# Graph network, mixer and routed experts on one core: the counting of the choices at seven turns' distance

## The chip, the cores and the metric

One NeuronCore of a Trainium2 chip runs the whole program in one launch. The metric is the device time of one execution, from its first to its last instruction, in microseconds. Three executions of the kernel before took 2806.68, 2806.97 and 2810.98 us; the median is 2806.97 us.

## What is computed

6250 nodes with 256 features pass three blocks, each added to the nodes; everything is float32:

```python
xn = _layernorm(x, axis=-1)
x = x + _L0_gnn_ref(xn, ...) + _L0_mix_ref(xn[None], ...)[0]
x = x + _L0_ffn_ref(_layernorm(x, axis=-1)[None], ...)[0]
# in _L0_ffn_ref, for E = 32 experts of hidden size 64:
logits = xf @ router_w.T + router_b
idx = jnp.argmax(logits, axis=-1)
h = relu(einsum('nd,ndh->nh', xf, W1[idx]) + b1[idx])
out = relu(einsum('nh,nhd->nd', h, W2[idx]) + b2[idx])
```

The first block averages edge features by node and puts them through two products; the second has four layers of linear attention and a feed-forward part; the third sends each node to the one expert with the highest logit.

## The kernel before, in words

The 6250 nodes stand as 50 tiles of 125; two tiles are a pair, and there are `GROUPS` = 25 pairs. The program goes through these stages: sorting and scattering of the edges beside the first mixer layer, the four mixer layers, the sums over the edges, then from about 2400 us **the routing loop**, and from about 2660 us the experts, which read whole pages of 128 tokens of one expert from a table in memory.

The routing loop is what the change touches. It is a pipeline written out by hand: each engine has a loop over turns i of its own (line 2433 for TensorE, 1951 for VectorE, 898 for GpSimd, and one for ScalarE), and `live(d)` says whether pair i-d exists. Work on pair i-d in turn i is at "distance d". The engines meet through semaphores only, and each handles its instructions in program order.

- Distance 0 to 2: `graph_input`, `graph_means`, `graph_transpose`, `graph_high`, `graph_low` bring a pair's inputs into the form `cT`; `graph_up(i-2, 0)` and `graph_up(i-2, 1)` make two chunks of hidden values (16 matmuls `cT_*,g_*` each) on TensorE. ScalarE makes `ghid` and its rounded part `ghh_hi`, VectorE the rest `ghh_lo` (`graph_hidden_low`, line 1834).
- Distance 3: `graph_down` (24 matmuls `g_*,ghh_*`). Distance 4: `graph_residual` adds the result to `res` (line 1839) and takes moments; GpSimd takes the root, VectorE the shift, ScalarE the normalised `zt`.
- Distance 5: TensorE transposes `zt` (line 2020), ScalarE copies it to `zT` (`route_copy`, line 1196). In ScalarE's turn this copy stands between `graph_relu(i-2, 0)` and `graph_hidden_high(i-2, 0)`.
- Distance 6: TensorE makes the logits (`rwT,zT`, eight matmuls), VectorE adds the bias (`logit`, line 1862), finds the largest and its index, and, as the last instruction of its turn, writes the choice as zeros and a one: `chosen` (line 1881). Four buffers `chosen[g % 4]` are in rotation.
- Distance 8: **the counting.** `rank_tokens` on TensorE adds up in a bank of PSUM how many tokens before each have chosen which expert (five small matmuls with `tri_r`, `ones_r` and `rest_r`); it stands at the head of TensorE's turn. VectorE reads the counts (`route_rank`: `limits`, line 1891, and `picks`, line 1892), computes the pages held (`route_pages`, line 1898), the ends of the pages, and picks the values for each token (`route_pick`, `route_sum`).
- Distance 9 on GpSimd: `token_slots` turns them into row numbers `fpos_i`, and `scatter_tokens` writes the pair's two tiles into the table by two indirect DMAs (line 894). For the last pairs, from `SLOTS_LATE` on, VectorE computes the row numbers itself, in the same turn (`route_slots`, last line 1943).

The order that these give to TensorE's turn, and what the counting products wait for:

```python
pe.wait_ge(n_chosen, g + 1)
pe.wait_ge(n_counted, COUNTED + g)
```

`n_chosen` is raised by `route_chosen(g)`, `n_counted` by `route_pages(g-1)`, since the bank keeps adding up and is read in between. The DMA of the pages' kinds on SP (line 738) waits for all 50 scatters, and the experts wait for that. VectorE's loop has 32 turns; from turn 27 on no new hidden chunks are left, and the last turns hold routing alone.

Of the kernel before, what the change touches and what calls it, by code (L numbers as in the profile page):

```python
# [21 lines left out]
GROUPS = TILES // PAIR  # L22
# [30 lines left out]
PAGE_RND = 8388608.0 * PAGE  # L53
FILL = 4
CHOICES = 4
SLOTS_LATE = GROUPS - 7
FSEGS = (N + EXP * (PAGE - 1)) // PAGE
RIN = 6

# [56 lines left out]
def build(nc, x, src, edge_attr, u, gW1, gb1, gW2, gb2, Wq, Wk, Wv, Wo, bo, ln1_g, ln1_b, mW1, mb1, mW2, mb2,  # L116
# [9 lines left out]
    with ctx:  # L126
# [409 lines left out]
        def pair(t, g, n=D):  # L536
            return t[:, bass.ds(g * PAIR, PAIR), 0:n]
# [208 lines left out]
        def _(pool):  # L746
# [145 lines left out]
            def scatter_tokens(g):  # L892
                for t in range(PAIR * g, PAIR * (g + 1)):
                    nc.gpsimd.indirect_dma_start(
                        out=tokens_sorted, out_offset=bass.IndirectOffsetOnAxis(ap=fpos_i[:, t:t + 1], axis=0),
                        in_=res[:, t, :], in_offset=None).then_inc(f_scat, 16)

            for i in range(4, GROUPS + 9):
                if i < GROUPS + 4:
                    pool.wait_ge(n_ve, i - 3)  # L900
                    nc.gpsimd.tensor_tensor(pair(res, i - 4, D + 1)[:, :, D], gve[:, :], tail_half[:, :], ALU.pow).then_inc(n_root, 1)
                if i == 9:
                    pool.wait_ge(blank_written, 32 + 16 * (KC + 1) * (FSEGS // FILL))
                if i >= 9:
                    token_slots(i - 9)
                    scatter_tokens(i - 9)

            for n in range(FSEGS):
                pool.wait_ge(f_row, n + 1)
# [340 lines left out]
        def _(dve):  # L1250
# [637 lines left out]
            def route_rank(g):  # L1888
                dve.wait_ge(n_ranked, g + 1)
                dve.wait_ge(n_placed, g)  # L1890
                step_(nc.vector.tensor_scalar(limits[:, :], PQT[0:P, PAIR * EXP:(PAIR + 1) * EXP], (PAGE - 1) / 2.0, PAGE_RND, ALU.add, ALU.add))
                step_(nc.vector.tensor_tensor(picks[:, :, 4, :], PQT[0:P, 0:PAIR * EXP].rearrange("p (j e) -> p j e", j=PAIR),
                                              chosen[g % CHOICES][:, :, :], ALU.mult))
# [7 lines left out]
            def route_ends(g):  # L1901
                stepped()
                step_(nc.vector.tensor_tensor_scan(ends[:, g % 2, :], ones[0:P, 0:EXP], fresh[:, :], ends[:, (g + 1) % 2, EXP - 1:EXP], ALU.mult, ALU.add))
# [44 lines left out]
            graph_x(0)  # L1948
            dve.wait_ge(gw_hi, 3)
            nc.vector.tensor_tensor(g2[1][:, :, :], raw_g2[:, :, :], f32(g2[0][:, :, :]), ALU.subtract).then_inc(gw_lo, 1)  # L1950
            for i in range(1, GROUPS + 8):
                def live(d):
                    return 0 <= i - d < GROUPS
                if live(4):
                    graph_residual(i - 4)
                if live(0):
                    graph_sums(i)
                if live(2):
                    graph_hidden_low(i - 2, 0)
                if live(0):  # L1960
                    graph_x(i)
                if live(4):
                    graph_shift(i - 4)
                if live(8):
                    route_rank(i - 8)
                if live(6):
                    route_logits(i - 6)
                if live(8):
                    route_pages(i - 8)
                if live(6):  # L1970
                    route_best(i - 6)
                if live(8):
                    route_ends(i - 8)
                if live(1):
                    graph_low(i - 1)
                if live(8):
                    route_grown(i - 8)
                if live(8):
                    route_book(i - 8)
                if live(6):  # L1980
                    route_index(i - 6)
                if live(8):
                    route_pick(i - 8)
                if live(2):
                    graph_hidden_low(i - 2, 1)
                if live(8):
                    route_sum(i - 8)
                    if i - 8 >= SLOTS_LATE:
                        route_slots(i - 8)
                if live(6):  # L1990
                    route_chosen(i - 6)

# [23 lines left out]
        def _(pe):  # L2016
# [413 lines left out]
            for k in range(KC):  # L2430
                nc.tensor.transpose(PQ[:, k * EXP:(k + 1) * EXP], rw_in[:, k * 128:(k + 1) * 128], ident[0:EXP, 0:EXP])
            nc.tensor.transpose(PQ[0:EH, KC * EXP:(KC + 1) * EXP], fb1_r, ident[0:EXP, 0:EXP]).then_inc(gcol_pe, 1)
            for i in range(2, GROUPS + 8):
                def live(d):
                    return 0 <= i - d < GROUPS
                if live(8):
                    rank_tokens(i - 8)
                if live(2):
                    graph_up(i - 2, 0)
                if live(6):  # L2440
                    route_logits(i - 6)
                if live(5):
                    route_transpose(i - 5)
                if live(2):
                    graph_up(i - 2, 1)
                if live(1):
                    graph_transpose(i - 1)
                if live(3):
                    graph_down(i - 3, 0)
                    graph_down(i - 3, 1)  # L2450
# [66 lines left out]
```

## Time and profile before

| | |
|---|---|
| median of three executions | 2806.97 us |
| the profiled execution: its own time | 2808.5 us |
| its span (first to last instruction recorded) | 2806.5 us |
| mean granted clock of TensorE | 0.968 |
| TensorE busy | 2623.6 us (93%) |
| VectorE busy | 2140.3 us (76%) |
| ScalarE busy | 1600.6 us (57%) |
| GpSimd busy | 1747.9 us (62%) |

Busy shares are means over stages with different limits. For one stage, the view of stretches gives each engine's busy time in it, and the timeline gives the single instructions in order; a bracket behind a row there tells how long the engine had been idle before it, and what released it. PE is TensorE, DVE VectorE, ACT ScalarE and POOL GpSimd. A granted clock of 1.00 is 2.4 GHz, 0.50 is 1.2 GHz.

### The profile page before, as it was taken

The page shows a single profiled execution, that of the slowest core. Times are in us where ns is not written, and L with a number is a line of the kernel's source. Part 1 is how long each engine was busy: PE and PEld are TensorE (multiplying, and loading weights), DVE is VectorE, ACT ScalarE, POOL GpSimd, SP SyncE. Part 2 cuts the span into 40 slices and gives each one's busy share as a digit, 9 for nine tenths or more (in the row PEclk, how much of TensorE's full clock was granted, in tenths as well). Part 3 has the DMA queues.
Part 4 walks back from the last instruction along what each step waited for, and adds up shares of the span by engine and source line. Part 5 has one row for each costly group of instructions (what it writes and reads, how often), then busy time and mean ns, then how long its engine had stood idle before and what let it go on. Part 6 is the DMA issues. An engine that isn't in the chain of part 4 may idle for free.

```text
span 2806.5 us, 57791 instructions
## 1 busy us (share of the span) xinstructions
PE 2623.6 (93%) x19601; PEld 2462.4 (88%) x19601; DVE 2140.3 (76%) x4920; ACT 1600.6 (57%) x3127; POOL 1747.9 (62%) x1751
## 2 busy tenths in 40 slices
PE   4888999999989999999999999989999999899798
PEld 3667899999979999998999999979998998899665
DVE  8988677777767777777677777778888888689754
ACT  0545466666646666664566666544444444677375
POOL 2145577777688877777887777745555555056555
PEclk7999999999999999999999999999999999899799
DMA  6012444334242322222422222234333332232252
GB/s 131 30 49 47 118 93 93 86 88 92 44 113 64 73 55 65 63 56 67 103 66 60 59 66 55 59 100 123 89 85 88 88 89 69 59 84 60 57 157 74
DMA packets 281805, 218.66 MB, mean 78 GB/s; under 512 B 171344, under 2 KB 220564, under 8 KB 281515
## 3 DMA queue, kind: packets, MB, share of 16 engines
q1 hardware_dynamic: 230444, 173.33, 23.8%
q0 software_dynamic: 51072, 41.66, 7.3%
q8 instruction: 160, 2.62, 0.4%
q14 instruction: 129, 1.06, 0.1%
HBM read 137.05 MB, written 80.92 MB: 78 GB/s over the span
## 4 chain that ended last, share of the span: by engine, by line
PE 66%; DVE 16%; issue 7%; POOL 7%; ACT 2%; DVEq 1%; DMA 1%; SPq 0%; POOLq 0%; ACTq 0%
PE bank L412 60%; POOL edges_sorted L812 5%; PE bank L2020 4%; DVE hidh_lo L1453 3%; DVE xh L1417 2%; DVE scr L1327 2%; DVE oh L1650 1%; PE bank L2488 1%; DVEq L1629 1%; POOL ehl L828 1%; DVE bn L1408 1%; DMA queries<-qn 1%; DVE bn_x L1253 1%; DVE res L1425 1%; POOL r L790 1%
## 5 line engine op out<-in xcount | busy, mean ns | idle before, releaser
L812 POOL DMA_INDIRECT edges_sorted<-staging,pos_i x850 | 1076.0, 1266 | 246.5 <-issue 230.1
L958 ACT ACTIVATE hid<-bank,b1p 128x250 f32<-128x250 f32 x800 | 331.6, 466 | 317.7 <-PE bank L412 315.5
L412 PE MATMUL bank<-w_hi,hidh_hi 128*125 128x256 f32 x1600 | 473.0, 296 | 23.1 <-DVE hidh_lo L1453 23.1
L412 PE MATMUL bank<-h_hi,w_hi 128*128 128x250 f32 x1600 | 479.3, 300 | 2.5 <-DVE h_lo L1437 2.4
L1453 DVE TENSOR_TENSOR hidh_lo<-hid,hidh_hi 128x500 fp32r<-128x500 f32 x400 | 319.7, 800 | 179.5 <-ACT hidh_hi L964 173.0
L412 PE MATMUL bank<-w_hi,hidh_lo 128*125 128x256 f32 x1600 | 454.2, 284 | 0.0
L412 PE MATMUL bank<-w_lo,hidh_hi 128*125 128x256 f32 x1600 | 452.6, 283 | 0.0
L412 PE MATMUL bank<-h_hi,w_lo 128*128 128x250 f32 x1600 | 448.8, 280 | 0.0
L412 PE MATMUL bank<-h_lo,w_hi 128*128 128x250 f32 x1600 | 445.3, 278 | 0.0
L412 PEld LDWEIGHTS bank<-w_hi,hidh_hi 128*125 128x125 f32 x1600 | 300.9, 188 | 32.1 <-DVE hidh_lo L1453 29.3
L964 ACT CAST hidh_hi<-hid 128x500 fp32r<-128x500 f32 x400 | 243.8, 610 | 122.6 <-PE bank L412 116.2
L412 PEld LDWEIGHTS bank<-h_hi,w_hi 128*128 128x128 f32 x1600 | 304.3, 190 | 6.5 <-DVE h_lo L1437 4.0
L412 PEld LDWEIGHTS bank<-h_lo,w_hi 128*128 128x128 f32 x1600 | 305.5, 191 | 1.9
L412 PEld LDWEIGHTS bank<-w_lo,hidh_hi 128*125 128x125 f32 x1600 | 300.5, 188 | 2.1
L412 PEld LDWEIGHTS bank<-h_hi,w_lo 128*128 128x128 f32 x1600 | 302.1, 189 | 0.0
L412 PEld LDWEIGHTS bank<-w_hi,hidh_lo 128*125 128x125 f32 x1600 | 300.3, 188 | 0.0
L790 POOL TENSOR_TENSOR r<-ve,minus_half 125x2 f32<-125x2 f32 x175 | 135.1, 772 | 217.1 <-DVE ve L1413 214.5
L828 POOL TENSOR_TENSOR ehl<-staging,ehl 128x512 fp32r<-128x512 f32 x103 | 137.6, 1336 | 148.5 <-ACT ehl L1050 136.2
L1650 DVE TENSOR_TENSOR oh<-iota_node,kb 128x1000 fp32r<-128x1000 f32 x153 | 190.3, 1244 | 43.5 <-POOL kb L823 43.3
L971 ACT COPY qT<-bank 128x500 f32<-128x500 f32 x100 | 57.7, 577 | 279.9 <-PE bank L2020 279.9
L412 PE MATMUL bank<-xh,ek 125*128 125x256 f32 x800 | 195.6, 390 | 6.7 <-DVE acc L1550 4.1
L412 PE MATMUL bank<-mmat,qT 128*125 128x256 f32 x800 | 191.8, 383 | 3.6 <-issue 3.6
(300 smaller groups left out, 6653.0 us busy)
## 6 DMA issues: line engine op xcount, KB each, us to landing
staging<-edges_sorted SPq DMA_DIRECT2D x103, 260.0 KB, 2.7
staging<-in_edge_attr SPq DMA_DIRECT2D x50, 531.2 KB
queries<-qn SPq DMA_DIRECT2D x100, 250.0 KB
qin<-queries SPq DMA_DIRECT2D x100, 250.0 KB
edges_sorted<-staging,pos_i POOLq DMA_INDIRECT x850
rows_in<-edges_sorted SPq DMA_DIRECT2D x50, 260.0 KB, 2.6
yin<-tokens_sorted SPq DMA_DIRECT2D x80, 130.0 KB, 2.1
tokens_sorted<-tri SPq DMA_DIRECT2D x40, 256.0 KB
```

The source lines that it names most:

```text
L412: return nc.tensor.matmul(o, left, right, start=start, stop=stop, skip_group_check=True)
L790: nc.gpsimd.tensor_tensor(o[:, :], ve[:, :], minus_half[:, :], ALU.pow).then_inc(done, 1)
L812: nc.gpsimd.indirect_dma_start(out=edges_sorted, out_offset=bass.IndirectOffsetOnAxis(ap=pos_i[:, i:i + 1], axis=0), in_=stage[:, slot, j, ...
L828: nc.gpsimd.tensor_tensor(ehl[n % 4][:, :, EA + 2:2 * EA + 2], rows_in[n % RIN][:, :, 0:EA], f32(ehl[n % 4][:, :, 0:EA]), ALU.subtract).th ...
L958: a = nc.scalar.activation(hid[c % 2][:, j, :], chunks(PH[c % 2])[:, j, :], ACT.Gelu, bias=b1p[:, 2 * c + j:2 * c + j + 1])
L964: nc.scalar.copy(hidh[c % 2][0][:, :, :], hid[c % 2][:, :, :]).then_inc(f_hi, 1)
L971: nc.scalar.copy(qT[:, :, :], chunks(PQT)).then_inc(q_copied, 1)
L1327: nc.vector.copy_predicated(pos_f[:, part], mask.bitcast(U16), PH[u % 2][0:P, 0:width]).then_inc(e_acc, 1)
L1417: a = nc.vector.tensor_scalar(o[:, j, :], res_row(PAIR * g + j), mv[:, j, 0:1], r[:, j:j + 1], ALU.subtract, ALU.mult)
L1453: nc.vector.tensor_tensor(hidh[c % 2][1][:, :, :], hid[c % 2][:, :, :], f32(hidh[c % 2][0][:, :, :]), ALU.subtract).then_inc(f_lo, 1)
L1650: nc.vector.tensor_tensor(oh[n % 4][:, :, :], iota_node[:, :].unsqueeze(1).to_broadcast((128, SEGR, P)), kb[:, n % 4, :].unsqueeze(2).to_b ...
L2020: a = nc.tensor.transpose(o[0:128, c, j * n:(j + 1) * n], i[:, j, c * 128:(c + 1) * 128], ident[0:n, 0:n])
```

## The change

The counting and all that stands behind it go from distance 8 to distance 7 on TensorE and VectorE, the slots and scatters from 9 to 8 on GpSimd; the loops of these three are one turn shorter. In TensorE's turn `rank_tokens` stands behind `graph_up(i-2, 0)` now, ahead of the logits. `SLOTS_LATE` goes from 18 to 19, so VectorE computes the row numbers of six pairs, and GpSimd those of nineteen. ScalarE's and SP's programs are the same.

```diff
-SLOTS_LATE = GROUPS - 7
+SLOTS_LATE = GROUPS - 6
...
-            for i in range(4, GROUPS + 9):
+            for i in range(4, GROUPS + 8):
...
-                if i == 9:
+                if i == 8:
                     pool.wait_ge(blank_written, 32 + 16 * (KC + 1) * (FSEGS // FILL))
-                if i >= 9:
-                    token_slots(i - 9)
-                    scatter_tokens(i - 9)
+                if i >= 8:
+                    token_slots(i - 8)
+                    scatter_tokens(i - 8)
...
-            for i in range(1, GROUPS + 8):
+            for i in range(1, GROUPS + 7):
...
-                if live(8):
-                    route_rank(i - 8)
+                if live(7):
+                    route_rank(i - 7)
                 if live(6):
                     route_logits(i - 6)
...
-            for i in range(2, GROUPS + 8):
+            for i in range(2, GROUPS + 7):
                 def live(d):
                     return 0 <= i - d < GROUPS
-                if live(8):
-                    rank_tokens(i - 8)
                 if live(2):
                     graph_up(i - 2, 0)
+                if live(7):
+                    rank_tokens(i - 7)
                 if live(6):
                     route_logits(i - 6)
```

`route_pages`, `route_ends`, `route_grown`, `route_book`, `route_pick`, `route_sum` and `route_slots` go from `live(8)` and `i - 8` to `live(7)` and `i - 7` in the same way, at their places in VectorE's turn.

**TensorE, a turn in the middle of the loop.** `chosen0` to `chosen3` are the four buffers of choices; `cT_*,g1_*` are products of `graph_up`, `g2_*,ghh*` of `graph_down`, `rwT,zT` the logits. Before, the last products of `graph_down` are followed by the counting, and that by `graph_up`:

```order
L412 MATMUL bank6<-g2_lo,ghh1_hi 125x256
L412 MATMUL bank6<-g2_hi,ghh1_lo 125x256
L412 MATMUL bank2<-chosen3,rest_r 125x64
L412 MATMUL bank2<-chosen3,ones_r 125x32
L412 MATMUL bank2<-chosen0,tri_r 125x64
L412 MATMUL bank2<-chosen0,ones_r 125x64
L412 MATMUL bank2<-chosen0,ones_r 125x32
L412 MATMUL bank4<-cT_hi,g1_hi 128x250
L412 MATMUL bank4<-cT_lo,g1_hi 128x250
```

With the change the counting stands behind the first half of `graph_up` and ahead of the logits:

```order
L412 MATMUL bank4<-cT_hi,g1_hi 128x250
L412 MATMUL bank4<-cT_hi,g1_lo 128x250
L412 MATMUL bank2<-chosen3,rest_r 125x64
L412 MATMUL bank2<-chosen3,ones_r 125x32
L412 MATMUL bank2<-chosen0,tri_r 125x64
L412 MATMUL bank2<-chosen0,ones_r 125x64
L412 MATMUL bank2<-chosen0,ones_r 125x32
L412 MATMUL bank3<-rwT,zT 125x32 x4
L2020 MATMUL bank1<-ident,zt 128x125 x4
```

These are the five products of pair 12 both times: they stand sixteen matmuls later in the turn now, and one turn earlier.

**TensorE, the last turns.** Before, the counting of pair 22 and the last logits, those of pair 24:

```order
L412 MATMUL bank2<-chosen1,rest_r 125x64
L412 MATMUL bank2<-chosen1,ones_r 125x32
L412 MATMUL bank2<-chosen2,tri_r 125x64
L412 MATMUL bank2<-chosen2,ones_r 125x64
L412 MATMUL bank2<-chosen2,ones_r 125x32
L412 MATMUL bank3<-rwT,zT 125x32 x4
L412 MATMUL bank2<-chosen2,rest_r 125x64
```

With the change, the same place:

```order
L412 MATMUL bank2<-chosen2,rest_r 125x64
L412 MATMUL bank2<-chosen2,ones_r 125x32
L412 MATMUL bank2<-chosen3,tri_r 125x64
L412 MATMUL bank2<-chosen3,ones_r 125x64
L412 MATMUL bank2<-chosen3,ones_r 125x32
L412 MATMUL bank3<-rwT,zT 125x32 x4
L412 MATMUL bank2<-chosen3,rest_r 125x64
```

The last logits stand behind the counting of pair 23 now, whose choice is buffer `chosen3`.

**VectorE, the end of the loop.** The last row numbers of the old turn 31, and what is left out behind them:

```order
 L1943 TENSOR_TENSOR fpos_i<-late_slots 125x2
-L1891 TENSOR_SCALAR limits<-bank 125x32
-L1892 TENSOR_TENSOR picks<-bank,chosen 125x2x32
-L1898 TENSOR_SCALAR book<-limits 125x32
-L1899 SCALAR_TENSOR_TENSOR fresh<-limits,book 125x32
-L1903 SCALAR_TENSOR_TENSOR ends<-ones,ends,fresh 125x32
-L1907 SCALAR_TENSOR_TENSOR fresh<-fresh,ends 125x32
-L1912 TENSOR_TENSOR book<-fresh,book 125x32
-L1917 TENSOR_TENSOR picks<-book,chosen 125x2x128
-L1927 TENSOR_REDUCE picked<-picks 125x10
-L1935 TENSOR_TENSOR late_slots<-picked 125x2 x2
-L1936 TENSOR_TENSOR late_slots<-picked 125x2
```

The loop's last turn is gone: the counting of pair 24 is VectorE's turn 31, in the place of pair 23's.

## Rows read from the trace of the kernel before

**Rows 1.** Busy time by stretch: us, each engine's busy us, PEclk, DMA share, GB/s
```profile
2250.00:2300.00 50.00, 46.20 (x378) 44.53 (x378) 42.61 (x64) 23.17 (x46) 28.93 (x33) 1.00 0.32 87
...
2550.00:2600.00 50.00, 50.00 (x451) 50.00 (x450) 45.63 (x176) 36.77 (x85) 31.12 (x63) 1.00 0.21 59
...
2639.00:2648.00 9.00, 3.00 (x18) 2.78 (x18) 8.07 (x48) 0.00 (x0) 6.02 (x6) 0.50 0.28 73
```

**Rows 2.** Timeline, TensorE, turn 19: start us, duration us, instruction, count
```profile
2553.04 0.96 PE L412 MATMUL bank<-rwT,zT 128*125 128x32 f32 x8
...
2553.83 0.63 PE L2020 MATMUL bank<-ident,zt 125*128 125x125 f32 x4
...
2559.65 0.19 PE L412 MATMUL bank<-chosen,rest_r 125*125 125x64 bf16 x1
...
2559.91 0.36 PE L412 MATMUL bank<-cT_hi,g_hi 128*128 128x250 f32 x1
...
2561.87 0.96 PE L412 MATMUL bank<-rwT,zT 128*125 128x32 f32 x8
```

**Rows 3.** Timeline, TensorE, the logits of turn 25
```profile
2606.02 0.96 PE L412 MATMUL bank<-rwT,zT 128*125 128x32 f32 x8
```

**Rows 4.** Timeline, ScalarE, turn 19 (in brackets: idle before, and releaser)
```profile
2554.50 0.58 ACT L1196 COPY zT<-bank 128x500 f32<-128x500 f32 x1 [0.42 <-PE bank L2020]
...
2554.97 0.61 ACT L1183 CAST ghh_odd_hi<-ghid 128x500 fp32r<-128x500 f32 x1
```

**Rows 5.** Timeline, VectorE, turn 19
```profile
2555.61 0.68 DVE L1834 TENSOR_TENSOR ghh_odd_lo<-ghid,ghh_odd_hi 128x500 fp32r<-128x500 f32 x1 [0.25 <-ACT ghh_odd_hi L1183]
...
2561.77 0.23 DVE L1881 TENSOR_TENSOR chosen<-iota_seg,res 125x64 bf16<-125x64 f32 x1
```

**Rows 6.** Timeline, VectorE, turns 25 to 32
```profile
2614.53 0.23 DVE L1881 TENSOR_TENSOR chosen<-iota_seg,res 125x64 bf16<-125x64 f32 x1
...
2623.00 0.23 DVE L1881 TENSOR_TENSOR chosen<-iota_seg,res 125x64 bf16<-125x64 f32 x1
...
2630.61 0.68 DVE L1839 TENSOR_TENSOR res<-res,bank 125x512 f32<-125x512 f32 x1
...
2637.86 0.23 DVE L1881 TENSOR_TENSOR chosen<-iota_seg,res 125x64 bf16<-125x64 f32 x1
...
2638.46 0.23 DVE L1862 TENSOR_TENSOR logit<-bank,rb_b 125x64 f32<-125x64 f32 x1
...
2638.60 0.17 DVE L1898 TENSOR_SCALAR book<-limits 125x32 f32<-125x32 f32 x1
...
2647.45 0.23 DVE L1881 TENSOR_TENSOR chosen<-iota_seg,res 125x64 bf16<-125x64 f32 x1
...
2647.59 0.18 DVE L1891 TENSOR_SCALAR limits<-bank 125x32 f32<-125x32 f32 x1
...
2650.80 0.16 DVE L1943 TENSOR_TENSOR fpos_i<-late_slots 125x2 int32<-125x2 f32 x1
...
2654.29 0.16 DVE L1943 TENSOR_TENSOR fpos_i<-late_slots 125x2 int32<-125x2 f32 x1
```

**Rows 7.** Timeline, TensorE, turns 27 to 30
```profile
2623.88 0.38 PE L412 MATMUL bank<-g_hi,ghh_hi 128*125 128x256 f32 x1 [1.33 <-DVE res L1839]
...
2628.34 0.19 PE L412 MATMUL bank<-chosen,rest_r 125*125 125x64 bf16 x1
...
2636.61 1.07 PE L2020 MATMUL bank<-ident,zt 125*128 125x125 f32 x4
...
2638.92 0.28 PE L412 MATMUL bank<-chosen,rest_r 125*125 125x64 bf16 x1 [1.24 <-DVE book L1898]
...
2639.23 0.37 PE L412 MATMUL bank<-chosen,ones_r 125*125 125x64 bf16 x2
...
2639.44 1.87 PE L412 MATMUL bank<-rwT,zT 128*125 128x32 f32 x8
```

**Rows 8.** Timeline, GpSimd, the scatter of the last pair
```profile
2654.75 1.19 POOL L894 DMA_INDIRECT tokens_sorted<-res,fpos_i  x1 [0.75 <-DVE fpos_i L1943]
```

More of the change, by code:

```diff
@@ L1963, in _ @@
                     graph_shift(i - 4)
-                if live(8):
-                    route_rank(i - 8)
+                if live(7):
+                    route_rank(i - 7)
                 if live(6):
                     route_logits(i - 6)
-                if live(8):
-                    route_pages(i - 8)
+                if live(7):
+                    route_pages(i - 7)
                 if live(6):
                     route_best(i - 6)
-                if live(8):
-                    route_ends(i - 8)
+                if live(7):
+                    route_ends(i - 7)
                 if live(1):
                     graph_low(i - 1)
[L1976 to L1979, printed above, removed]
+                if live(7):
+                    route_grown(i - 7)
+                if live(7):
+                    route_book(i - 7)
                 if live(6):
                     route_index(i - 6)
-                if live(8):
-                    route_pick(i - 8)
+                if live(7):
+                    route_pick(i - 7)
                 if live(2):
                     graph_hidden_low(i - 2, 1)
[L1986 to L1989, printed above, removed]
+                if live(7):
+                    route_sum(i - 7)
+                    if i - 7 >= SLOTS_LATE:
+                        route_slots(i - 7)
                 if live(6):
@@ L2432, in _ @@
             nc.tensor.transpose(PQ[0:EH, KC * EXP:(KC + 1) * EXP], fb1_r, ident[0:EXP, 0:EXP]).then_inc(gcol_pe, 1)
-            for i in range(2, GROUPS + 8):
+            for i in range(2, GROUPS + 7):
                 def live(d):
                     return 0 <= i - d < GROUPS
-                if live(8):
-                    rank_tokens(i - 8)
                 if live(2):
                     graph_up(i - 2, 0)
+                if live(7):
+                    rank_tokens(i - 7)
                 if live(6):
```

## The prediction

> **What bounds the kernel now.** I read the stretches of 50 us first. From 2450 to 2600 us the routing loop runs, and in such a stretch TensorE is busy 50.00 of 50 us at a granted clock of 1.00, while VectorE has 45.63 [rows 1]. So a turn costs what TensorE issues in it. The marks of one turn show the length: the logits of turn 19 start at 2553.04 and those of turn 20 at 2561.87, 8.83 us later [rows 2]; turn 25 has them at 2606.02 [rows 3], and 52.98 us for six turns is 8.83 again. The loop's end is different: from 2639 to 2648 us VectorE is busy 8.07 of 9.00 us and TensorE 3.00, at half its clock [rows 1]. There the chain of waits runs through VectorE, turn by turn, to the last row numbers at 2654.29; GpSimd waits for these, 0.75 us idle, before its scatter at 2654.75 [rows 6, 8], and the expert pages are loaded behind that. What counts is therefore whether the loop keeps 8.83 us a turn, and when the last row numbers are written.
>
> **The part that decides: a choice needed sooner than it is made.** In the new order the counting products of pair i-7 stand in TensorE's turn i behind `graph_up(i-2, 0)`, where the logits start now. They need the choice of that pair, which VectorE writes as its last routing step of turn i-1. Followed through one turn of the old trace: the logits start at 2553.04, the transposes of `zt` at 2553.83 [rows 2]. ScalarE waited 0.42 us for these and copies at 2554.50, and only behind this copy, at 2554.97, does it round the hidden chunk [rows 4]. VectorE waited 0.25 us for that and starts at 2555.61; from there its own row of work leads to the choice, 2561.77 + 0.23 = 2562.00 [rows 5]. That is 8.96 us after the logits began and 0.13 us after the logits of the next turn began [rows 2]. Before, the choice had a whole further turn; now TensorE stands and waits for it.
>
> It is not a wait paid once, since it closes a ring. Counting products of turn i, then logits and transposes, ScalarE's copy and rounding, VectorE's chain to the choice, counting products of turn i+1. The ring's length is the sum of its pieces: the five counting products, 0.26 us from 2559.65 to 2559.91 [rows 2], now ahead of the logits; the 8.96 us; and the way from VectorE to TensorE, 0.15 us, as VectorE's held pages end at 2638.77 and the products that wait for them start at 2638.92 [rows 6, 7]. The sum is 9.37 us, **0.54 us more than 8.83**. TensorE has 0.54 us less to do than the ring lasts, and stands idle by that in each turn. The choice of pair 1, counted in turn 8, is the first that comes behind counting work on VectorE; so turns 7 to 25 are the ring's marks, 18 lengths: 18 x 0.54 = 9.7 us. The next length is shorter, as VectorE has no new pair to add there: from 2606.02 to the choice at 2614.53 + 0.23 is 8.74 us, with 0.41 it is 9.15, another 0.3 us [rows 3, 6]. From turn 26 the ring is left, but its counting products remain between the chunk and the transposes: 0.26 us. By then VectorE is **10.3 us** late. Were the way to TensorE to cost nothing, the loop's part would be 0.15 x 19 = 2.9 us less; that is the lower bound.
>
> By the Trainium skill, page "Perfetto Trace Analysis", section "Identifying the Most-Contended Engine", the engine to look at is the one with the highest occupancy, TensorE by how long it loads weights; in this stretch its loads fill 50.00 of 50 us [rows 1], the products are the same before and after, and a turn would stay at 8.83 us. That is the rival "no ring" below. The rows agree with the rule for the old order only.
>
> **The end of the loop.** One turn goes: the last row numbers came 2654.29 - 2650.80 = 3.49 us after the ones before [rows 6], work that TensorE's old distance had put into a turn of its own. **-3.49 us.** Against it stand new waits. In turns 29 to 31 VectorE begins with the counts, and the choice they rest on is its last work of the turn before. Before, it went from the choice (2647.45) to `limits` (2647.59) in 0.14 us [rows 6]. Now the choice must end (0.23), reach TensorE (0.15), be counted (2638.92 to 2639.23 + 0.37, so 0.68) [rows 7] and come back (0.04, as ScalarE starts at 2554.50 behind transposes that end at 2553.83 + 0.63) [rows 2, 4]: 1.10 us, **+0.96**. In turns 29 and 30 it is more, because the logits stand behind the counting products in TensorE's queue: they start 0.52 us after these and take 1.87 us at half clock [rows 7], so VectorE has them 0.23 + 0.15 + 0.52 + 1.87 + 0.04 = 2.81 us after the choice began, where it was 2638.46 - 2637.86 = 0.60 [rows 6]: **2 x 2.21 us**. All counts, 4.42 + 0.96 - 3.49 = **+1.9 us**. At full clock (0.96 us for the logits [rows 2], 0.26 for the counts) these turns would wait 1.04, 1.04 and 0.54 us, and the end would gain 0.9 us; the clock in this stretch is 0.50 [rows 1], so I take +1.9.
>
> In turn 27 TensorE does the last `graph_down`, which now also stands behind the counts. It had waited 1.33 us at 2623.88, and lasted until 2628.34 [rows 7]. The choice of turn 26, at 2623.00 + 0.23, comes 10.3 us later, so counts, logits and transposes start at 2633.7 and end 1.9 us (0.26 + 0.96 + 0.63) to 3.5 us (0.52 + 1.87 + 1.07) later; with 4.46 us for the products they are done at 2640.1 to 2641.7. VectorE adds the result at 2630.61 + 10.3 = 2640.9 [rows 6]. Late by 0 to 0.8 us; I take **+0.4**.
>
> **What costs nothing.** GpSimd's slots and both scatters of a pair move one turn earlier, past the root of the next pair; its distance to VectorE's counting is the same, and its last scatter waited for row numbers, not for the queue [rows 8]. Pair 18's slots are computed by GpSimd in place of VectorE, ten instructions for seven, beside a turn that VectorE or TensorE sets; if the cover is gone it is late by these small instructions once. VectorE's turn 7 gets counting work that fills idle time. SP issues the same loads in the same order, and the five products are the same ones.
>
> **Sum.** 10.3 + 0.4 + 1.9 = +12.6 us. Against the profiled execution, 2808.5 us, that is 2821.1; this execution is 1.5 us above the median of the runs, 2806.97, so against that I predict **2819.6 us**.
>
> **Rivals.**
> - *No ring* (the other side: not slower). If the choice is released before its record's end, or VectorE closes up so that TensorE hardly waits, the loop stays at 8.83 us and only the end is left: -3.5 us if its waits are hidden, +1.9 if not, so 2803 to 2809 us, no measurable change. It decides from the point where the ring is within 0.17 us of the turn (18 x 0.17 + 2.3 is 5.4 us). For it speaks only the smallness of 0.54 us; against it that ScalarE's 0.42 and VectorE's 0.25 us of waiting [rows 4, 5] show both standing behind TensorE already.
> - *The clock falls in the loop.* Each idle piece of 0.54 us could take the granted clock down to its half level. Then logits take 0.91 us more, counts 0.26 and transposes 0.44 [rows 2, 7], all on the ring: 1.6 us x 18 = 29 us more, 2849 us; half of that if it falls in some turns. Against it, from 2250 to 2300 us TensorE was busy only 46.20 of 50 us, a larger idle share than 0.54 of 9.37, and the clock stayed at 1.00 [rows 1]. The Trainium skill, "TensorE: Matmul & The Clock Gate", section "A second HAM failure mode: psum-queue depth-cycling", tells of a kernel whose clock went up and down because TensorE paused often and briefly between groups; by it this rival would come true, and the row of 2250 us speaks against it.
> - *The ring is shorter than summed*, with 0.1 to 0.3 us a turn left: 2811 to 2815 us. This joins the forecast, as its lower part.
>
> **How the numbers follow.** The forecast, with the shorter ring, gets 0.77; the clock 0.07; no ring 0.16, of which 0.03 is a gain of over 0.2%, should the end and something behind it gain together. A change within 0.2%, 5.6 us, is about what a measurement of this kernel can't tell from none. So slower 0.84, less 0.02 for a ring so short that it is not told: 0.82; same 0.15; faster 0.03. The range runs from 2811 us (ring 0.3 us, or no way to TensorE and full clock at the end) to 2829 us (the clock falling in a third of the turns): it leaves out most of "no ring" and the upper clock case, together just under 2 in 10.
>
> **What would show it.** Right: the logits of successive turns 9.3 to 9.4 us apart; an idle piece of about 0.5 us of TensorE before each first counting product, released by VectorE's choice; TensorE's busy time near 47 of 50 us at clock 1.00; in the last three turns VectorE idle about 1 us before `limits`, in two of them 1 to 2 us more before `logit`; six late turns of slots on VectorE in place of seven. Wrong: turns still of 8.83 us, or a clock under 0.95 between 2450 and 2600 us.

## The result, and the profile after

| | before | after |
|---|---|---|
| median, us | 2808.93 (2806.68 to 2812.97, 7 runs) | 2818.08 (2815.11 to 2824.44, 7 runs) |
| the profiled execution, us | 2808.5 | 2815.11 |
| its span, us | 2806.5 | 2813.1 |
| mean granted clock of TensorE | 0.968 | 0.972 |

The change makes the kernel slower: a ratio of 1.0034, with an interval of 1.0021 to 1.0047, which is 6 to 13 us. The median is 1.5 us below the predicted 2819.6 us. Part of that closeness is luck: the forecast was 12.6 us on top of a median of 2806.97 us (three executions), and the median of seven is 2808.93 us, so the change costs 9.2 us where 12.6 were forecast. The parts below show where the rest went.

Busy time by stretch, kernel after (us, then TensorE, weight loads, VectorE, ScalarE and GpSimd, granted clock, DMA share, GB/s):

```profile
2550.00:2600.00 50.00, 48.35 (x424) 47.35 (x423) 43.11 (x170) 35.78 (x84) 30.35 (x65) 1.00 0.19 54
2640.00:2650.00 10.00, 3.31 (x17) 2.92 (x17) 7.08 (x43) 0.72 (x2) 3.88 (x4) 0.50 0.20 54
```

From 2550 to 2600 us TensorE was busy 50.00 us before, with 451 matmul instructions [rows 1]; now it is 48.35 us with 424. The clock is 1.00 in both. VectorE and ScalarE do less per stretch as well: no engine is full, and each of them waits for another. The turn shows for whom. Timeline of TensorE, kernel after (in brackets: idle before, and releaser):

```profile
2451.47 0.24 PE L412 MATMUL bank<-chosen,rest_r 125*125 125x64 bf16 x1 [0.36 <-DVE chosen L1881]
...
2554.01 0.28 PE L412 MATMUL bank<-cT_hi,g_lo 128*128 128x250 f32 x1
2554.60 0.24 PE L412 MATMUL bank<-chosen,rest_r 125*125 125x64 bf16 x1 [0.31 <-DVE chosen L1881]
...
2554.91 1.04 PE L412 MATMUL bank<-rwT,zT 128*125 128x32 f32 x8
...
2563.98 0.24 PE L412 MATMUL bank<-chosen,rest_r 125*125 125x64 bf16 x1 [0.32 <-DVE chosen L1881]
...
2610.87 0.24 PE L412 MATMUL bank<-chosen,rest_r 125*125 125x64 bf16 x1 [0.35 <-DVE chosen L1881]
...
2620.05 0.24 PE L412 MATMUL bank<-chosen,rest_r 125*125 125x64 bf16 x1
```

Here `rest_r` is the first of the five counting products. It waits for `chosen` in each turn. From the mark at 2451.47 to the one at 2610.87 are 17 lengths, 159.40 us: **9.376 us a turn**, where it was 8.83 [rows 2, 3].

The way round the ring, after the logits of 2554.91: ScalarE, then VectorE.

```profile
2556.45 0.58 ACT L1196 COPY zT<-bank 128x500 f32<-128x500 f32 x1 [1.29 <-PE bank L2020]
2556.92 0.61 ACT L1183 CAST ghh_odd_hi<-ghid 128x500 fp32r<-128x500 f32 x1
```

```profile
2557.56 0.68 DVE L1834 TENSOR_TENSOR ghh_odd_lo<-ghid,ghh_odd_hi 128x500 fp32r<-128x500 f32 x1 [0.83 <-ACT ghh_odd_hi L1183]
...
2563.69 0.23 DVE L1881 TENSOR_TENSOR chosen<-iota_seg,res 125x64 bf16<-125x64 f32 x1
```

ScalarE's wait before the copy was 0.42 us and is 1.29; VectorE's before `ghh_odd_lo` was 0.25 and is 0.83 [rows 4, 5]. Each engine stands behind the one ahead of it in the ring.

The end of the loop, timeline of VectorE, kernel after:

```profile
2628.53 0.23 DVE L1881 TENSOR_TENSOR chosen<-iota_seg,res 125x64 bf16<-125x64 f32 x1
...
2636.08 0.68 DVE L1839 TENSOR_TENSOR res<-res,bank 125x512 f32<-125x512 f32 x1
...
2643.39 0.23 DVE L1881 TENSOR_TENSOR chosen<-iota_seg,res 125x64 bf16<-125x64 f32 x1
2644.42 0.19 DVE L1891 TENSOR_SCALAR limits<-bank 125x32 f32<-125x32 f32 x1 [0.81 <-PE bank L412]
...
2646.12 0.23 DVE L1862 TENSOR_TENSOR logit<-bank,rb_b 125x64 f32<-125x64 f32 x1 [1.38 <-PE bank L412]
...
2656.72 0.23 DVE L1881 TENSOR_TENSOR chosen<-iota_seg,res 125x64 bf16<-125x64 f32 x1
...
2660.97 0.16 DVE L1943 TENSOR_TENSOR fpos_i<-late_slots 125x2 int32<-125x2 f32 x1
```

Before, `limits` came 0.14 us after the choice began, and `logit` without a wait [rows 6]. Now the three last turns of VectorE wait 0.81 us for the counts, and two of them 1.38 us more for the logits. One turn less stands behind them.

**A ruler that all runs share.** TensorE's transposes of `an` run from the loop's first turn to its 25th. The first and the last of them, and the last `fpos_i`, cut each trace into a loop, an end of the loop, and the rest. The group of these transposes, kernel before, then kernel after (count, ns, first and last start):

```profile
L2367 PE MATMUL bank<-ident,an x50: 270/270/415, 2400.2 to 2609.7; 125*128 125x125 f32 x50
```

```profile
L2367 PE MATMUL bank<-ident,an x50: 270/270/415, 2396.9 to 2614.9; 125*128 125x125 f32 x50
```

The loop lasts 209.5 us before and 218.0 after; the end 44.6 (to 2654.29) and 46.1 (to 2660.97); the rest 152.2 and 152.1. The same numbers for all kernels of this study, each of one profiled execution:

| kernel | loop begins | loop, us | end, us | rest, us | turn, us | ratio to before, interval |
|---|---|---|---|---|---|---|
| before | 2400.2 | 209.5 | 44.6 | 152.2 | 8.83 | 1 |
| after | 2396.9 | 218.0 | 46.1 | 152.1 | 9.38 | 1.0034 (1.0021 to 1.0047) |
| e1_behind_transposes | 2405.3 | 208.2 | 43.0 | 152.2 | 8.84 | 0.9995 (0.9986 to 1.0004) |
| e2_choice_sooner | 2410.5 | 207.9 | 42.5 | 152.3 | 8.83 | 0.9995 (0.9986 to 1.0004) |
| e3_choice_sooner_behind | 2403.5 | 208.1 | 42.2 | 153.6 | 8.84 | 0.9995 (0.9986 to 1.0004) |
| e4_copy_later | 2408.1 | 213.4 | 45.7 | 152.2 | 9.19 | 1.0029 (1.0017 to 1.0041) |
| f1_middle_at_8 | 2408.0 | 207.6 | 44.6 | 152.2 | 8.83 | 1.0002 (0.9992 to 1.0012) |
| f2_head_at_7 | 2403.0 | 296.2 | 49.6 | 153.8 | 12.80 or 14.22, mean 13.67 | 1.0322 (1.0300 to 1.0344) |
| f3_low_later | 2406.3 | 220.6 | 46.4 | 152.2 | 9.43 | 1.0043 (1.0028 to 1.0059) |
| f4_copy_low_later | 2406.5 | 206.9 | 45.3 | 152.3 | 8.83 | 1.0005 (0.9996 to 1.0015) |

The code ahead of the loop is the same in all ten, and yet the loop begins anywhere from 2396.9 to 2410.5 us. A single span is therefore worth little here; the loop, the end and the turn are what the traces tell apart. The kernel before was timed anew beside each set of experiments: 2814.89 us (29 runs) beside e1 to e4, 2815.07 us (21 runs) beside f1 to f4. The ratios of e1 to f4 are to these, that of the change to its own 2808.93 us.

### The profile page after: what moved, and what is told of

The parts are those of the page before. It is cut to its first block, busy times and chain, and to the rows that moved or that the text cites. A ratio compares the mean times of both kernels' runs of the same rounds, so it can differ in the third digit from the quotient of the medians.

```text
span 2813.1 us, 57794 instructions
## 1 busy us (share of the span) xinstructions
PE 2618.4 (93%) x19601; PEld 2454.0 (87%) x19601; DVE 2137.2 (76%) x4913; ACT 1599.5 (57%) x3127; POOL 1746.2 (62%) x1760
## 4 chain that ended last, share of the span: by engine, by line
PE 64%; DVE 19%; issue 8%; POOL 4%; ACT 2%; DVEq 1%; DMA 1%; SPq 0%; ACTq 0%; POOLq 0%
PE bank L412 58%; PE bank L2020 4%; DVE hidh_lo L1453 3%; POOL edges_sorted L812 3%; DVE xh L1417 2%; DVE scr L1327 1%; DVE oh L1650 1%; PE bank L2488 1%; DVEq L1629 1%; POOL ehl L828 1%; DMA queries<-qn 1%; DVE bn L1408 1%; DVE bn_x L1253 1%; DVE res L1425 1%; DVE kmask L1312 1%
## 5 line engine op out<-in xcount | busy, mean ns | idle before, releaser
L1650 DVE TENSOR_TENSOR oh<-iota_node,kb 128x1000 fp32r<-128x1000 f32 x153 | 190.3, 1243 | 42.2 <-POOL kb L823 42.0
```

The source lines that it names most:

```text
L1650: nc.vector.tensor_tensor(oh[n % 4][:, :, :], iota_node[:, :].unsqueeze(1).to_broadcast((128, SEGR, P)), kb[:, n % 4, :].unsqueeze(2).to_b ...
```

## The experiments

Three theories. **Ring**: the counting products need the choice of the turn before, and this closes a ring of 9.37 us. **Place**: the middle of TensorE's turn is itself a bad place for them. **Scatter**: the loop is not the cause; the stages ahead of it differ from one execution to the next, and that is the loss.

**e1: counting behind the transposes.** Against the changed kernel, in TensorE's turn. The distance stays at seven; only logits and transposes leave the ring's way.

```diff
-                if live(7):
-                    rank_tokens(i - 7)
                 if live(6):
                     route_logits(i - 6)
                 if live(5):
                     route_transpose(i - 5)
+                if live(7):
+                    rank_tokens(i - 7)
```

> Distance 7 as in the change, but the counting products stand behind the transposes of zt, 1.42 us later in TensorE's turn (2553.04 to 2553.83 and 0.63 more). Ring theory (choice to counts to logits, transposes, ScalarE, VectorE, choice, 9.37 us long, is what lengthened the turn): the logits and transposes no longer stand behind the choice, which comes 0.13 + 0.15 us after the logits begin and so before its place in the queue. Turns go back to 8.83 us, no idle piece of TensorE in the loop, 0.96 us of wait in each of the last three turns against the 3.49 us turn that is gone: about 0.6 us under the kernel before, near 2808, and 10 us under the change. Place theory (what costs is small products in the middle of TensorE's turn, pushing later work of the turn back): they are still in the middle, turns stay over 9.3 us, 2818. Scatter theory (the loop is not the cause, the stages ahead of it differ from run to run): 2818 again, whatever the turns do.

Measured: 2813.12 us (2810.72 to 2815.74, 11 runs). Timeline of TensorE, e1:

```profile
2540.03 0.19 PE L412 MATMUL bank<-chosen,rest_r 125*125 125x64 bf16 x1
...
2548.87 0.19 PE L412 MATMUL bank<-chosen,rest_r 125*125 125x64 bf16 x1
```

8.84 us apart, with no wait. The choice is still VectorE's last work of the turn, and is counted in the very next; what went is that logits and transposes stand behind the count in TensorE's queue. The end keeps a wait for the counts, and loses the one for the logits:

```profile
2647.81 0.19 DVE L1891 TENSOR_SCALAR limits<-bank 125x32 f32<-125x32 f32 x1 [0.81 <-PE bank L412]
...
2656.45 0.16 DVE L1943 TENSOR_TENSOR fpos_i<-late_slots 125x2 int32<-125x2 f32 x1
```

**e2: the choice sooner.** Against the changed kernel, in VectorE's turn; TensorE as changed.

```diff
                 if live(6):
                     route_index(i - 6)
+                if live(6):
+                    route_chosen(i - 6)
                 if live(7):
                     route_pick(i - 7)
...
-                if live(6):
-                    route_chosen(i - 6)
```

> The change with the counting where it put it, but VectorE writes the choice of pair i-6 right behind its index, ahead of picks, the second hidden chunk and the sum: 1.33 us sooner in the loop (2560.25 to 2561.58) and 1.86 us in the last turns (2635.81 to 2637.67). Ring theory: the ring is 9.37 - 1.33 = 8.04 us, shorter than TensorE's 8.83, so turns are 8.83 us and TensorE does not wait; in the last turns the counts arrive in time and the logits 0.35 us late in two of them, so the end gives 3.49 - 0.7: 2.8 us under the kernel before, about 2806. Place theory: TensorE's order is the change's own, so 9.37 us a turn and 2818. Scatter theory: 2818.

Measured: 2813.58 us (2812.62 to 2816.01, 11 runs), turns of 8.83 us. Now the counting stands in the middle of TensorE's turn exactly as in the change, at the same distance, and costs nothing: this speaks against Place. VectorE's work is the same in sum; only the piece from `route_pick` to `route_slots` (with the second hidden chunk's `ghh_lo`) has left the ring. Timeline of TensorE, e2:

```profile
2543.79 0.19 PE L412 MATMUL bank<-chosen,rest_r 125*125 125x64 bf16 x1
...
2552.61 0.19 PE L412 MATMUL bank<-chosen,rest_r 125*125 125x64 bf16 x1
```

**e3: both edits.**

> Both edits together: choice right behind its index, counting products behind the transposes. Ring theory: 8.83 us a turn and in the last turns no wait for counts or logits, so the whole 3.49 us of the turn that is gone: about 2805.4, 0.12% under the kernel before and 13 us under the change. If the waits in the last turns are set by something else than the place of logits and choice, it equals the run with only the choice moved. Place theory and scatter theory: 2818.

Measured: 2813.18 us (2809.43 to 2816.86, 11 runs), turns of 8.84 us, and the shortest end of all, 42.2 us; VectorE no longer waits for counts or logits in it. Timeline of VectorE, e3:

```profile
2650.54 0.19 DVE L1891 TENSOR_SCALAR limits<-bank 125x32 f32<-125x32 f32 x1 [0.46 <-DVE fpos_i L1943]
...
2653.76 0.16 DVE L1943 TENSOR_TENSOR fpos_i<-late_slots 125x2 int32<-125x2 f32 x1
```

The end is 2.4 us shorter than before, in the trace, where 3.49 were expected; part of the missing 1.1 us are three casts (line 1877) of 0.44 to 0.45 us in the last turns, usually 0.16, and 0.46 us idle ahead of the last `limits`, which the trace puts down to VectorE's own `fpos_i`. The measured ratio, 0.9995, is 1.4 us with an interval of 3.9 us less to 1.1 us more: the gain of 3.5 us is within it, but not shown, and the times of e1, e2 and e3 can't be told apart. In e3's trace 1.4 us are lost again behind the last row numbers: in the 30 us that follow the first `zs` transposes the clock is 0.94, against 1.00 before, and the rest is 153.6 us against 152.2.

**e4: the copy out of the ring.** Against the changed kernel, in ScalarE's turn. This attacks the ring where the prediction had followed it: VectorE's `graph_hidden_low` waits for the rounding, which waits behind `route_copy`.

```diff
-                if live(5):
-                    route_copy(i - 5)
                 if live(2):
                     graph_hidden_high(i - 2, 0)
+                if live(5):
+                    route_copy(i - 5)
+                if live(2):
                     graph_relu(i - 2, 1)
```

> The change, with ScalarE's copy of zT moved behind its rounding of the first hidden chunk; TensorE's and VectorE's orders are the change's own. It tells whether the ring closes through that copy. Ring theory: the rounding can start once the hidden values are there, some 0.95 us sooner, and nothing behind the counting products stands ahead of VectorE's chain any more; the choice is 8.0 us behind the start of the logits and the turn is 8.83 us. The end keeps its waits (1.2 us more than it saves), so about 2810. Place theory: 9.37 us a turn, 2818. A ring that closes through VectorE alone would also stay at 9.3 us or more.

Measured: 2823.51 us (2820.91 to 2825.10, 6 runs), a ratio of 1.0029 (1.0017 to 1.0041). Turns of 9.19 us, not 8.83: **my expectation fell**. The wait for `ghh_hi` is gone, and a new one is there. Timelines of TensorE, ScalarE and VectorE in one turn, e4 (in e4 and f4, lines behind the moved copy have numbers one higher):

```profile
2562.32 0.24 PE L412 MATMUL bank<-chosen,rest_r 125*125 125x64 bf16 x1
...
2571.52 0.24 PE L412 MATMUL bank<-chosen,rest_r 125*125 125x64 bf16 x1
```

```profile
2566.05 0.83 ACT L1172 ACTIVATE ghid<-bank,g1col 128x250 f32<-128x250 f32 x2 [1.30 <-PE bank L412]
...
2567.23 0.39 ACT L1165 CAST cT_hi<-bank 128x250 fp32r<-128x250 f32 x1
```

```profile
2567.65 0.68 DVE L1830 TENSOR_TENSOR cT_lo<-bank,cT_hi 128x500 fp32r<-128x500 f32 x1 [0.58 <-ACT cT_hi L1165]
```

A reading of these rows: a second way leads round. Behind counts, logits and transposes TensorE makes the second chunk (`graph_up(·, 1)`), ScalarE's `graph_relu(·, 1)` waits 1.30 us for it and has `graph_high` behind it, VectorE's `graph_low` waits 0.58 us for `cT_hi`, and the choice stands behind `graph_low`. From the count at 2562.32 to the next at 2571.52 are 9.20 us. Against the changed kernel's 9.38 us this way is 0.18 us the shorter one, and it could not be seen there: `cT_lo` starts without a wait. f4 tests this reading.

**f1: the middle, at eight turns' distance.** Against the kernel before.

```diff
-                if live(8):
-                    rank_tokens(i - 8)
                 if live(2):
                     graph_up(i - 2, 0)
+                if live(8):
+                    rank_tokens(i - 8)
```

> The kernel before with the counting products of group i-8 moved from the head of TensorE's turn to the middle (behind graph_up of the first half), the distance of eight turns kept. Ring theory (the loss needs the distance of seven, because only then does a turn's count wait for a choice made in the same turn): the choice is a turn older, so no wait at the counting products, turns of 8.83 us, 209 to 210 us from the first to the last transposes of the graph's sums (before 209.6), a ratio of 1.000 within 0.001. Place theory (the middle of the turn is itself the bad place, by the bank's reuse or by breaking up TensorE's row): turns of 9.2 to 9.4 us as in the change, 218 us over that stretch, a ratio of 1.003 to 1.004.

Measured: 2814.68 us (2812.74 to 2818.33, 10 runs), a ratio of 1.0002; turns of 8.83 us. TensorE has in the five places of its turn what the changed kernel has there, and only the distance differs. Place is out: half of the change, alone, costs nothing.

```profile
2549.83 0.19 PE L412 MATMUL bank<-chosen,rest_r 125*125 125x64 bf16 x1
...
2558.66 0.19 PE L412 MATMUL bank<-chosen,rest_r 125*125 125x64 bf16 x1
```

**f2: the other half, seven turns' distance with the counting at the head.** Against the changed kernel.

```diff
+                if live(7):
+                    rank_tokens(i - 7)
                 if live(2):
                     graph_up(i - 2, 0)
-                if live(7):
-                    rank_tokens(i - 7)
```

> The changed kernel with the counting products of group i-7 at the head of TensorE's turn. Ring theory: graph_up's first half (1.95 us) now lies inside the ring between the counting products and the logits, so the ring is 0.26+1.95+8.96+0.15 = 11.3 us; turns of 11.3 us, +2.5 us in each of 18 turns over before, +45 to +50 us with the end, at a clock that stays at 1.00; each turn TensorE stands idle 2 to 2.5 us for chosen. If the clock falls under such gaps, more: turns of 12 to 13 us and +65 us or more. Place theory, in which the middle is what costs: turns of 8.8 to 8.9 us as before, and a ratio of 1.000.

Measured: 2905.52 us (2 runs), +90 us, a ratio of 1.0322 (1.0300 to 1.0344). The direction is the Ring's and Place is wrong again; the size is not that of the 45 to 50 us, and is above the upper case in its turns (12 to 13 us expected, 13.67 on average measured). There are two kinds of turn, 11 of 14.2 us and 7 of 12.8 us between the marks of turns 8 and 26; the rows show one of each. Timeline of TensorE, then busy time by stretch, f2:

```profile
2526.52 0.24 PE L412 MATMUL bank<-chosen,rest_r 125*125 125x64 bf16 x1 [2.03 <-DVE chosen L1881]
...
2529.67 1.73 PE L412 MATMUL bank<-rwT,zT 128*125 128x32 f32 x8
...
2540.74 0.24 PE L412 MATMUL bank<-chosen,rest_r 125*125 125x64 bf16 x1 [2.01 <-DVE chosen L1881]
...
2544.35 1.16 PE L412 MATMUL bank<-rwT,zT 128*125 128x32 f32 x8
...
2553.54 0.24 PE L412 MATMUL bank<-chosen,rest_r 125*125 125x64 bf16 x1 [2.20 <-DVE chosen L1881]
```

```profile
2530.30:2532.90 2.60, 2.60 (x14) 2.60 (x14) 0.00 (x0) 1.02 (x4) 1.93 (x5) 0.50 0.02 6
...
2540.70:2542.50 1.80, 1.76 (x13) 1.76 (x14) 1.69 (x5) 0.00 (x0) 0.00 (x0) 0.68 0.29 112
2542.50:2544.40 1.90, 1.90 (x11) 1.90 (x11) 0.36 (x2) 0.00 (x0) 1.54 (x7) 0.50 0.00 0
2544.40:2547.00 2.60, 2.60 (x24) 2.60 (x24) 0.00 (x0) 1.82 (x4) 2.04 (x6) 0.93 0.00 0
2547.00:2549.00 2.00, 2.00 (x20) 2.00 (x19) 1.74 (x7) 1.21 (x4) 1.59 (x1) 1.00 0.24 58
```

The second turn is 12.80 us. Behind an idle piece of 2.0 us the granted clock goes to 0.50, and with it the work that I had put at 2.21 us (counts and `graph_up(·, 0)`) takes 3.61 us, from 2540.74 to 2544.35; the rest of the ring, 9.19 us, is almost the sum of before. The first turn is 14.22 us: the clock is still 0.50 from 2530.30 to 2532.90, behind the start of the logits. The logits take 1.73 us in place of 1.16, and from their start to the next count are 11.07 us in place of 9.19. The 18 turns are 87 us longer than at 8.83 us, which is nearly all of the +90. A ring that leaves TensorE idle for 2 us a turn here also slows what is on the ring.

**f3: `graph_low` later, the control for f4.** Against the changed kernel, in VectorE's turn.

```diff
-                if live(1):
-                    graph_low(i - 1)
                 if live(7):
                     route_grown(i - 7)
                 if live(7):
                     route_book(i - 7)
+                if live(1):
+                    graph_low(i - 1)
```

> The changed kernel with VectorE's graph_low(i-1) moved behind route_grown and route_book, nothing else. Control for the next. In the changed kernel as it is, the ring goes through ScalarE's copy and rounding to graph_hidden_low, which stands ahead of all of these, so their order behind it is the same sum: turns of 9.37 us, the wait of 0.83 us for ghh_hi on VectorE unchanged, a ratio to before of 1.003 to 1.004. If the ring were closed through graph_low already (cT_hi), turns would fall to 9.0 us or less.

Measured: 2827.23 us (2825.06 to 2829.32, 4 runs), a ratio of 1.0043 (1.0028 to 1.0059); turns of 9.43 us, with the wait for `ghh_hi` as it was:

```profile
2550.36 0.68 DVE L1834 TENSOR_TENSOR ghh_odd_lo<-ghid,ghh_odd_hi 128x500 fp32r<-128x500 f32 x1 [0.83 <-ACT ghh_odd_hi L1183]
...
2556.55 0.23 DVE L1881 TENSOR_TENSOR chosen<-iota_seg,res 125x64 bf16<-125x64 f32 x1
```

With the first ring closed, the order behind `ghh_lo` gains nothing. It even costs 0.06 us: from `ghh_odd_lo` to the choice are 6.19 us here and 6.13 in the changed kernel. I had expected the same sum; small instructions that need each other's result now stand side by side, which may be the reason, and was not tried by itself.

**f4: both ways round opened.** e4 and f3 together.

> ScalarE's route_copy behind its graph_hidden_high (which alone gave turns of 9.19 us in place of the expected 8.83) and VectorE's graph_low(i-1) behind route_grown and route_book. Second-ring theory (with the copy out of the way the ring closes through TensorE's graph_up second half, ScalarE's relu and cT_hi, and VectorE's graph_low, which waits 0.58 us for cT_hi): 0.40 to 0.45 us of VectorE's work now goes ahead of that wait, the second ring is 9.19-0.4 = 8.8 us, and turns are 8.83 to 8.85 us, 209 us over the transposes' stretch, a ratio of 0.999 to 1.001. Rival (the copy's later place costs by itself, as zT comes later for the logits or the bank comes free later): turns stay at 9.2 us, 213.5 us over the stretch, a ratio of 1.002 to 1.003.

Measured: 2817.34 us (2812.08 to 2820.22, 10 runs), a ratio of 1.0005 (0.9996 to 1.0015). Timeline of TensorE, f4:

```profile
2547.63 0.19 PE L412 MATMUL bank<-chosen,rest_r 125*125 125x64 bf16 x1
...
2556.44 0.19 PE L412 MATMUL bank<-chosen,rest_r 125*125 125x64 bf16 x1
```

The two are 8.81 us apart, the 18 turns around them 8.83 on average, and there is no wait before the counts: the later place of the copy costs nothing by itself, and `graph_low` later, which costs a little alone, gives back all that e4 had left. The second ring is shown. f4 also isolates the end: its turns are not longer, it keeps the waits of 0.81 and 1.39 us, and its end is 45.3 us, 0.7 more than before.

The theory of Scatter expected 2818 us for e1, e2 and e3, whatever their turns do; they came out at 0.9995 of the kernel before, with the stages ahead of the loop unchanged, and the longer turn stands inside the loop. Nor is GpSimd behind the loss, whose scatters are now a turn nearer to the loop's end: in the changed kernel it waits for VectorE ahead of them. Timeline of GpSimd, kernel after:

```profile
2656.90 1.19 POOL L894 DMA_INDIRECT tokens_sorted<-res,fpos_i  x1 [3.98 <-DVE fpos_i L1943]
...
2661.42 1.19 POOL L894 DMA_INDIRECT tokens_sorted<-res,fpos_i  x1 [1.85 <-DVE fpos_i L1943]
```

## Why the prediction was right, and where it was not

**The ring: right, and its pieces nearly so.** Predicted 0.26 + 8.96 + 0.15 = 9.37 us, measured 9.376. The pieces after: counting products to logits 0.31 us (2554.60 to 2554.91); logits to the end of the choice 9.01 us (to 2563.69 + 0.23 = 2563.92); and the next count at 2563.98, 0.06 us after that end. So the five products are 0.05 us dearer when TensorE has just stood still (their first lasts 0.24 us, against 0.19 [rows 2]), the way from the logits to the choice is 0.05 longer (from the logits to the transposes of `zt` it is 0.87 us behind the counting, 2554.91 to 2555.78, and was 0.79 [rows 2]), and the way from VectorE to TensorE was put 0.09 us too high. That price came from another pair, `book` and the count behind it [rows 6, 7]; from `chosen` to the count it is 0.06 us in the loop and 0.05 in its end at half clock (2656.72 + 0.23 to 2657.00), so the clock is not what made 0.15. That these errors took each other away is luck. The rival "ring is shorter" was right in this one piece and not in the sum.

**The idle piece is not the loss.** I had expected about 0.5 us idle before each count; the trace has 0.31 to 0.37, though each turn lasts 0.54 us longer. Matmuls overlap: the last record before the gap starts at 2554.01 and lasts 0.28, but its follower would have started about 0.12 us after it, the pace of the others. From 2554.13 to 2554.60 are 0.47 us, and 0.05 for the dearer counts make 0.52. The busy share shows it no better, 48.35 of 50 us where 0.54 of 9.38 would leave 47.1. The distance between marks is what is to be read.

**Turns 25 and 26: right.** 2610.87 to 2620.05 is 9.18 us, predicted 9.15; VectorE's choices of turns 25 and 26 are 8.76 us apart where it was 8.47 [rows 6], +0.29. From the count of turn 26 to the choice of turn 26 the change adds 0.33, for a predicted 0.26. VectorE is 10.5 us later in the loop, for a predicted 10.3.

**The end: sign right, size half.** From the choice of turn 26 to the last row numbers were 31.29 us and are 32.44: **+1.15**, where the two terms had 1.9 + 0.4 = +2.3. The term of 0.4 for `graph_down` was wrong: `res` starts at 2636.08, 5.47 us later than at 2630.61 [rows 6], and the choice of turn 26 is 5.53 us later; nothing is late between. The last products of `graph_down` end at 2633.5 us in the changed kernel, 2.6 us before `res`: there 23 of the 24 take 0.28 or 0.29 us each, where 15 took 0.41 before. The others: turn 29 +1.64, turn 30 +2.10, turn 31 +0.90, the turn that is gone -3.49. Predicted were 2.21 and 2.21 and 0.96 in sum with -3.49. The difference is mostly in turn 29, where the kernel before has a cast of 0.59 us in place of the usual 0.16. It is no chance of one execution: f1, which counts at eight turns' distance too, has the same cast at the same length in the same turn, and the changed kernel has it at 0.16. Timelines of GpSimd and VectorE, kernel before, then f1:

```profile
2641.68 1.19 POOL L894 DMA_INDIRECT tokens_sorted<-res,fpos_i  x1 [0.30 <-issue]
2642.25 0.59 DVE L1877 CAST res<-besti 125x2 f32<-125x2 uint32 x1
```

```profile
2647.62 1.19 POOL L894 DMA_INDIRECT tokens_sorted<-res,fpos_i  x1 [0.30 <-issue]
2648.19 0.59 DVE L1877 CAST res<-besti 125x2 f32<-125x2 uint32 x1
```

Both casts start while GpSimd has a scatter under way and end 0.03 us before it does (2642.84 and 2642.87 us, 2648.78 and 2648.81), and so, within 0.04 us, do the casts of 0.42 to 0.45 us in the last turns of e2 and e3. Casts of 0.16 us overlap scatters as well, so what decides is not shown. The old turn 29 held 0.43 us that the new order does not pay, and the sum had added its waits to a turn with them in it. So the missing 1.15 us are 0.4 of `graph_down`, 0.43 of this cast, and 0.3 over three turns, which fits the way to TensorE put 0.1 us too high each time. Waits and clock are as argued: 0.81 + 1.38 us, at 0.50.

**What no step had: the stages around.** Ring and end give about +11.6 us (9.8 for the lengths up to the count of turn 25, 0.35 and 0.33 for the next two pieces, 1.15), and the profiled spans differ by 6.6. The 5 us between are ahead of the ring, in turns that hold no counting yet. The loop begins 3.3 us sooner in the trace after; and from there to the place where the counting of turn 7 begins, the first of all, it takes 45.3 us, where the logits of turn 7 came after 47.0 before; the clock is 0.94 in place of 0.87 in these 50 us. These are the rows of 2400 to 2450 us, kernel before, then after:

```profile
2400.00:2450.00 50.00, 45.54 (x351) 44.85 (x351) 28.80 (x73) 33.87 (x81) 2.81 (x4) 0.87 0.32 77
```

```profile
2400.00:2450.00 50.00, 47.57 (x387) 47.34 (x388) 30.21 (x88) 35.88 (x86) 2.80 (x4) 0.94 0.28 67
```

Over the ten profiles the loop's begin scatters by 13.6 us and its length up to the logits of turn 7 by 2.8 (44.3 to 47.1), both more than this, so I take it for chance of one execution; that was argued, not tried. The medians differ by 9.2 us, between 6.6 and 11.6.

**The rivals.** "No ring" fell with the 9.38 us; by the rule of the Trainium skill, "Perfetto Trace Analysis", section "Identifying the Most-Contended Engine", TensorE was the engine to look at, judged by its weight loads. In the kernel after it is still the fullest, with loads in 47.35 of 50 us where VectorE has 43.11, and does not set the turn: the measurement decides. "The clock falls" did not come true in the change: 0.31 us idle in each turn leave the clock at 1.00, while the 2.0 us of f2 are followed by 0.50. By the Trainium skill, "TensorE: Matmul & The Clock Gate", section "A second HAM failure mode: psum-queue depth-cycling", short pauses again and again can bring the clock down and up. In the change, with pauses of 0.31 to 0.37 us, the rows speak against it, and in f2, with pauses of 2.0 to 2.2 us, they agree.

**What the prediction had not seen:** the ring it named was the longer of two, 9.38 and 9.19 us. For the change this made no difference, as the longest sets the turn; for a repair it does, since e4, aimed at the named one alone, won 0.19 of 0.54 us.

## What to carry to other kernels

An engine that is busy 50.00 of 50 us is no warrant that a turn keeps its length. When the distance of a step is cut by a turn, add up the way from its result back to its own start in the next turn, over all engines and their program orders; if the sum passes the turn, the difference is paid in every turn, and no busy share names it. Look for a second way round before repairing the first, and cut where all ways pass: here that is the choice itself (e2), or what stands behind the count on TensorE (e1). A saved turn of 3.49 us at the end was worth 1.6 to 2.4 us in the traces (e1, e2, e3), and only once at least the new waits for the logits were gone; in the times it is not told from nothing.

## What the runs showed that was not expected

- The counting products cost 0.31 us after a stop and 0.26 in a row of matmuls.
- From the end of `chosen` on VectorE to the start of the count that waits for it are 0.06 us in the loop and 0.05 in its end, at half clock; from `book` to the count that waits for it are 0.15. The way from one engine to another depends on the instruction at its start; why is open.
- An idle piece of 2.0 to 2.2 us per turn takes the clock to 0.50 right behind it. In one turn of f2 this is from 2542.5 to 2544.4 us, and it is back at 1.00 from 2547 us; in others it lasts longer, so there are turns of 12.8 and of 14.2 us. The 0.31 to 0.37 us of the changed kernel leave it at 1.00.
- A cast on VectorE that usually lasts 0.16 us lasts 0.42 to 0.59 us in the loop's end, in four of the ten traces, and then ends with a scatter of GpSimd.
- Ten profiled executions begin the loop within 13.6 us of each other, after the same code. That is more than the effect under study.
